# Attention kernel on one core: P times V of two blocks in a row at every second block, with four buffers of exponentials instead of two

## The chip, the core and the metric

The kernel runs on one core of a Trainium2 chip. The core has a matrix engine (PE, TensorE), a vector engine (DVE, VectorE), an activation engine (ACT, ScalarE), a general engine (POOL, GpSimd) and DMA queues (issued here by SP, SyncE). The engines run their own instruction streams in order and meet at semaphores. PE writes its products to PSUM, which has eight banks of 2 KB per partition; DVE and ACT read them from there. The metric is the device time of one execution in microseconds; before the change it is 294.55 us (median of 3 runs, 294.25 to 294.76).

## The reference, cut to what matters

Input x is 4 batches x 512 tokens x 128 channels, in fp32.

```
xn  = layernorm(x)
q   = (xn @ Wq + bq)            as 16 heads of 8
k   = ((xn @ Wk + bk) @ Wl + bl) as 16 heads of 8
v   = ((xn @ Wv + bv) @ Wl + bl) as 16 heads of 8
att = softmax(q k^T / sqrt(8)) @ v       for each batch and head
x   = x + layernorm(att @ Wo + bo)
# then a gated feed-forward part with a shift by one token
xr, xk = mu*xn + (1-mu)*previous token of xn      (xn = layernorm(x))
x   = x + layernorm(sigmoid(xr @ W_r^T) * (square(relu(xk @ W_k^T)) @ W_v^T))
```

## The kernel before

A batch has 16 heads in 4 groups (GH = 4 heads each) and 512 keys in 4 tiles of 128. A block is one group and one key tile: 16 blocks per batch (BLK = 16, block n has group n // 4 and tile n % 4), 64 blocks in all. In the text, E(0) to E(3) are the four score products of a block for its exponentials, one per head (`scores_for_exponentials`, line 1262: 128 keys x 512 queries, in bf16). They go to the two banks of psB in turn. X(0) to X(3) are the four exponentials of ACT (line 784), which read these banks and write pT, of which there are two buffers, one per block. M stands for the four score products for the maxima (`scores_for_maxima`, line 1243), which are done LEAD = 6 blocks ahead of their use. Two of them (u = 0) fill the first half of psA, two (u = 1) the second, and DVE takes the maximum over each half in one reduction: R(0) and R(1) (line 933). After four blocks POOL splits the maxima of a group into three bf16 parts in four steps (`split_maxima`, lines 493, 553, 557), PE transposes them (job "m"), ACT copies them and a DMA brings them into QS.

PV is `times_v` (line 1274): for one block, four products, one per head, of V (128 keys x 32 columns, of which 8 are the head's and one holds ones for the row sum) with pT (128 keys x 512 queries), in fp32. Each writes 32 partitions of the bank psO, and the four tiles of a group add up there. The chip has two matmul instructions for each of these fp32 products, so that a block's PV is eight in the trace: four column tiles, then the four again. After a group ACT copies psO to o_sb (`take_o`), PE transposes it (job "on") and DVE divides by the sums (`normalise`).

The order is written out by hand. On PE a block is

E(0), M, E(1), M, M, E(2), M, E(3), then PV of the block before.

Between these stand the jobs, by the table PE_AT with pairs (block, place): the transposes of the outputs of a group ("on"), of the maxima ("m"), and those of the feed-forward part of the batch before ("oT", "y", "x1T", "r", "kf", "f"). Place 0 is after the first half of M, place 1 after the third M, 2 after the fourth, 3 after E(3) and ahead of PV, 4 after PV. ACT_AT and DVE_AT set the same for the other engines: ACT does X(0), X(1), results, X(2), X(3) with results also ahead of X(0); DVE does R(0), work, R(1), work.

The waits that matter here are these. E(i) waits until the exponential two before it has been done (`e_rdy`), since psB has two banks. The first M of a half waits until the reduction of that half of the block before is done (`a_max`). X of block n waits until PV of the last block that used its pT buffer is done (`pv_done`). PV waits for the exponentials of its block (`e_rdy`), at a group's first tile also for V (`vg_rdy`) and for the copy of the group before out of psO (`o_tak`). For the last six blocks of the last batch there are no more M, and psA serves as two further banks for E.

Batch 0 has no feed-forward jobs, batches 1 and 2 run in a loop, the last is written out again.

Of the kernel before, what the change touches and what calls it, by code (L numbers as in the profile page):

```python
# [23 lines left out]
def sandwich_kernel(nc, x, Wq, bq, Wk, bk, Wv, bv, Wl, bl, Wo, bo, W_r, W_k, W_v, mu_r, mu_k, out):  # L24
# [4 lines left out]
    ACT = mybir.ActivationFunctionType  # L29
# [3 lines left out]
    NB, T, E = x.shape  # L33
    H = 16
    D = E // H
    P = 128
    NT = T // P
    GH = 4
    NG = H // GH
    BLK = NG * NT  # L40
# [11 lines left out]
    with ctx:  # L52
        def sb(name, shape, dt=fp32):
            return ctx.enter_context(nc.sbuf_tensor(name, shape, dt))
# [4 lines left out]
        def sem(name):  # L59
            return ctx.enter_context(nc.semaphore(name))  # L60
# [50 lines left out]
        MC = GH * NT  # L111
        mm = sb("mm", [P, P], bf16)
        mmT = sb("mmT", [PARTS * MC, P], bf16)
        pT = sb("pT", [P, 2, GH, T])
        o_sb = sb("o_sb", [P, T])
        rsum = sb("rsum", [P, NT, GH])
        oq = sb("oq", [P, NT, H, D])
# [106 lines left out]
        pv_done = sem("pv_done")  # L224
# [117 lines left out]
        def job_before(b, job, first, last):  # L342

            have = [j for j in JOBS if not (first and j[0] == "F") and not (last and j[0] == "L")]
            at = [j[1] for j in have].index(job)
            if not at:

                return (m_tak, 1) if first else (on_tak, b * NG - 1)
            _, _, taken, a, c = have[at - 1]
            return taken, b * a + c  # L350

        def later(n):

            return not isinstance(n, int) or n > 0
# [3 lines left out]
        def score_bank(n, i, last):  # L358

            if last and n >= TAIL and i >= 2:  # L360
                return psA[:, 0, i - 2, :]
            return psB[:, i % 2, :]
# [319 lines left out]
        def _(act):  # L682
# [54 lines left out]
            for t in range(NT):  # L737
                last = nc.scalar.copy(bout[:, t, :], psA[:, 1, 1, 0:E])
            last.then_inc(s_boc, 1)
            def take_first_maxima(_):  # L740
                take_maxima(0, psB[:, 0, :].bitcast(bf16))
# [36 lines left out]
            def exponentials(b, n, i, last):  # L778

                act.wait_ge(b_rdy, b * (BLK * GH) + (n * GH + i + 1))  # L780
                if n >= 2 or later(b):

                    act.wait_ge(pv_done, b * BLK + (n - 1))
                nc.scalar.activation(pT[:, n % 2, i, :], score_bank(n, i, last), ACT.Exp,  # L784
                                     scale=SCALE).then_inc(e_rdy, 1)

            def batch(b, first, last):
                for n in range(BLK):
                    take_results(b, n, 0, first, last)
                    exponentials(b, n, 0, last)  # L790
                    exponentials(b, n, 1, last)
                    take_results(b, n, 1, first, last)
                    exponentials(b, n, 2, last)
                    exponentials(b, n, 3, last)
# [60 lines left out]
            for u in range(2):  # L855
                act.wait_ge(z_fst, 2 * HALF * (u + 1))
                for t in z_tiles(u):
                    last = nc.scalar.activation(zf[:, t, :], f_sb[:, t, :], ACT.Identity, scale=-1.0,
                                                bias=mv_f[:, t, 0:1])
# [290 lines left out]
        def _(pe):  # L1150
# [52 lines left out]
            def job_m(n, bank=psM_b):  # L1203
                pe.wait_ge(m_p2, n + 1)
                nc.tensor.transpose(bank[:, 0:P], mm[:, :], ident_b[:, :]).then_inc(m_rdy, 1)  # L1205

            def job_on(n):
                pe.wait_ge(o_tak, n + 1)
                transposes(lambda t: o_sb[:, P * t:P * (t + 1)], on_rdy)
# [26 lines left out]
            def scores_for_maxima(e, a, g, h, u, j, free=False):  # L1236

                if u == 0 and j == 0 and h == 0:
                    pe.wait_ge(ld[g], (e + 1) * (16 * LW))
                if j == 0 and not free:  # L1240
                    pe.wait_ge(a_max, a * 2 + (u - 1))
                t = 2 * u + j
                score = nc.tensor.matmul(psA[:, u, j, :], QS[g][0:KMAX, h, P * t:P * (t + 1)],  # L1243
                                         KS[g][0:KMAX, h, :], start=True, stop=True)
                if j == 1:
                    score.then_inc(a_rdy, 1)

            def scores_for_exponentials(b, n, i, later_tile, last):

                g, t = n // NT, n % NT  # L1250
                if t == 0 and i == 0:
                    pe.wait_ge(m_in, b * (16 * NG) + 16 * (g + 1))
                if last and n >= TAIL and i >= 2 and n == TAIL:
                    if i == 2:
                        pe.wait_ge(a_max, 2 * BLK * NB)
                elif last and (n > TAIL or n == TAIL and i >= 2):

                    pe.wait_ge(e_rdy, b * (BLK * GH) + (n * GH + i - 3))
                elif later_tile:

                    pe.wait_ge(e_rdy, b * (BLK * GH) + (n * GH + i - 1))
                nc.tensor.matmul(score_bank(n, i, last), KS[g][0:KEXP, i, P * t:P * (t + 1)],  # L1262
                                 QS[g][0:KEXP, i, :], start=True, stop=True).then_inc(b_rdy, 1)

            def times_v(b, n, later_group):

                g, t = n // NT % NG, n % NT
                if t == 0:
                    pe.wait_ge(vg_rdy, b * NG + (n // NT + 1))
                    if later_group:  # L1270
                        pe.wait_ge(o_tak, b * NG + n // NT)
                pe.wait_ge(e_rdy, b * (BLK * GH) + GH * (n + 1))
                for i in range(GH):
                    last = nc.tensor.matmul(psO[QUAD * i:QUAD * (i + 1), :], Vg[:, g, t, i, :],  # L1274
                                            pT[:, n % 2, i, :], start=(t == 0), stop=(t == NT - 1))
                last.then_inc(pv_done, 1)

            job_xT(0)
# [2 lines left out]
            for j in range(2):  # L1281
                nc.tensor.matmul(psA[:, 1, 0, E * j:E * (j + 1)], w_T[:, T_WK + j, :], w_in[:, WL, :],
                                 start=True, stop=True).then_inc(s_wkl, 1)
            job_q(0)
            pe.wait_ge(s_vec, 16 * 7)
            for j in range(2):
                nc.tensor.matmul(psA[:, 1, 1, j:j + 1], w_in[:, WL, :], vec[:, V_BK + j:V_BK + j + 1],
                                 start=True, stop=True).then_inc(s_bkl, 1)
# [8 lines left out]
                             stop=True).then_inc(s_bo, 1)  # L1297
# [27 lines left out]
            def batch(b, first, last):  # L1325
                def jobs(n, place):

                    for kind, name, _, _, _ in JOBS:
                        if PE_AT[name] == (n, place) and not (first and kind == "F") \
                                and not (last and kind == "L"):  # L1330
                            pe.wait_ge(*job_before(b, name, first, last))
                            run_job(name)

                def run_job(name):
                    if name.startswith("on"):
                        job_on(b * NG + int(name[2:]))
                    elif name.startswith("m"):
                        job_m(b * NG + int(name[1:]))
                    else:
                        {"oT": job_oT, "y": job_y, "x1T": job_x1T, "r": job_r, "kf": job_kf,  # L1340
                         "f": job_f}[name](b - 1)

                for n in range(BLK):
                    ahead = n + LEAD

                    def for_maxima(u, j):
                        if ahead < BLK or not last:
                            scores_for_maxima(b + ahead // BLK, b * BLK + ahead, ahead // GH % NG,
                                              ahead % GH, u, j)

                    def for_exponentials(i):
                        scores_for_exponentials(b, n, i, i > 1 or n > 0 or not first, last)

                    for_exponentials(0)
                    for_maxima(0, 0)
                    for_exponentials(1)
                    for_maxima(0, 1)
                    jobs(n, 0)
                    for_maxima(1, 0)
                    jobs(n, 1)  # L1360
                    for_exponentials(2)
                    for_maxima(1, 1)
                    jobs(n, 2)
                    for_exponentials(3)
                    if first and n == 0:
                        pe.wait_ge(k_tak, 2 * NB)
                        pe.wait_ge(q_tak, 2 * NB)
                    jobs(n, 3)
                    if n or not first:
                        times_v_before(b, n, first)  # L1370
                    jobs(n, 4)

            def times_v_before(b, n, first):
                if n:
                    times_v(b, n - 1, n > 1 or not first)
                else:
                    times_v(b - 1, BLK - 1, True)

            batch(0, True, False)
            with pe.Fori(1, NB - 1) as i:  # L1380
                batch(i, False, False)
            batch(NB - 1, False, True)
            e = NB - 1
            times_v(e, BLK - 1, True)


# [79 lines left out]
```

## Time and profile before

| | |
|---|---|
| time, median of 3 runs | 294.55 us |
| span of the profiled execution, first to last instruction | 292.1 us |
| PE busy | 257.6 us, 88% of the span |
| DVE busy | 218.2 us, 75% |
| ACT busy | 180.4 us, 62% |
| POOL busy | 108.1 us, 37% |
| 512 PV matmuls (line 1274), busy together | 69.1 us |
| 128 reductions for the maxima (line 933), mean of one | 1216 ns |
| 244 exponentials (line 784), mean of one | 597 ns |

The page gives no time of the profiled execution other than its span, which is 2.45 us shorter than the median of the runs. Matmuls overlap: one takes about 0.38 us from its start to its end, but the next one starts 0.22 us after it, so starts say more than durations. In the timeline a row stands for several instructions in a row where it says x2 or more; its time is from the first start to the last end.

### The profile page before, as it was taken

Reading aid. Unit: us, or ns where it says so; the run is one execution under the profiler, and the core shown is the slowest. Engines: PE = TensorE matmul, PEld = TensorE weight load, DVE = VectorE, ACT = ScalarE, POOL = GpSimd, SP = SyncE. Lnnn points to the kernel's source line nnn. Section 1 sums busy time; section 2 is a strip of 40 time slices with the busy share of each in tenths; the row PEclk is TensorE's granted clock in tenths of the full one; section 3 lists DMA queues with packets and bytes.
Section 4 is the critical chain, followed back from the end, with each engine's and each line's share of the span. In section 5 each row is a group of like instructions: output and inputs, shape, how many; then the busy total and the mean of one; then the engine's idle time right before and its main releaser. Section 6 shows DMA issues by size and latency. Waiting matters only on the chain.

```text
span 292.1 us, 4845 instructions
## 1 busy us (share of the span) xinstructions
PE 257.6 (88%) x1379; PEld 100.2 (34%) x1379; DVE 218.2 (75%) x384; ACT 180.4 (62%) x351; POOL 108.1 (37%) x236
## 2 busy tenths in 40 slices
PE   7764883099999999999999999999999999898980
PEld 2441541022323232432433334233333433333560
DVE  2695494065888787989889889988998988763545
ACT  2334350566787867687776776777677678695041
POOL 4897370321001011066321344552117155324522
PEclk9686699558999999999999999999999999999798
DMA  4331133160111111110101121010102000000101
GB/s 108 108 109 77 77 125 123 52 198 2 61 39 66 42 46 56 33 77 19 68 27 57 33 88 49 33 66 20 68 12 103 17 1 2 4 1 0 36 2 36
DMA packets 13045, 15.64 MB, mean 54 GB/s; under 512 B 2529, under 2 KB 10722, under 8 KB 13026
## 3 DMA queue, kind: packets, MB, share of 16 engines
q1 hardware_dynamic: 12450, 15.15, 15.5%
q10 hardware_dynamic: 576, 0.26, 0.3%
q8 instruction: 9, 0.15, 0.2%
q14 instruction: 10, 0.08, 0.1%
HBM read 11.01 MB, written 4.19 MB: 52 GB/s over the span
## 4 chain that ended last, share of the span: by engine, by line
PE 72%; DMA 9%; DVE 8%; SPq 4%; ACT 3%; issue 3%; POOL 1%; POOLq 0%; DVEq 0%; ACTq 0%
PE psO L1274 20%; PE psB L1262 20%; PE psA L1243 17%; DMA q_scr<-qp 4%; DVE mx L933 4%; PE psM L1167 3%; PE psM L1173 3%; SPq L382 3%; DMA KS<-k_scr 3%; PE psA L1154 2%; PE psB L1396 1%; DVE er L996 1%; DMA x_all<-in_L_attn_x_dram 1%; PE psO L1186 1%; SPq L401 1%
## 5 line engine op out<-in xcount | busy, mean ns | idle before, releaser
L933 DVE TENSOR_REDUCE mx<-psA 128x2 f32<-128x1024 f32 x128 | 150.8, 1216 | 45.2 <-PE psA L1243 44.8
L784 ACT ACTIVATE pT<-psB 128x512 f32<-128x512 f32 x244 | 133.1, 597 | 41.2 <-PE psB L1262 40.4
L1262 PE MATMUL psB<-QS,KS 99*128 99x512 bf16 x244 | 94.7, 393 | 12.3 <-DMA QS<-mmT 11.9
L1243 PE MATMUL psA<-KS,QS 96*128 96x512 bf16 x256 | 90.7, 391 | 5.7 <-DMA KS<-k_scr 4.4
L1274 PE MATMUL psO<-pT,Vg 128*32 128x512 f32 x512 | 69.1, 611 | 0.4
L1262 PEld LDWEIGHTS psB<-QS,KS 99*128 99x128 bf16 x244 | 23.6, 98 | 92.0 <-ACT pT L784 57.3
L1243 PEld LDWEIGHTS psA<-KS,QS 96*128 96x128 bf16 x256 | 25.2, 100 | 28.7 <-DVE mx L933 6.2
L493 POOL TENSOR_TENSOR mm<-mx,one 128x16 bf16<-128x16 f32 x16 | 3.5, 217 | 43.2 <-DVE mx L933 43.2
L1274 PEld LDWEIGHTS psO<-pT,Vg 128*32 128x32 f32 x512 | 10.2, 108 | 21.8 <-issue 16.9
L532 POOL TENSOR_TENSOR Vg<-v_st,one 128x128 f32<-128x128 f32 x16 | 6.3, 399 | 28.0 <-PE psO L1274 28.0
L703 ACT ACTIVATE qf<-psO,vec 128x512 f32<-128x512 f32 x4 | 2.7, 687 | 18.0 <-DMA q_scr<-qp 13.4
L1154 PE MATMUL psA<-warm 128*128 128x512 bf16 x36 | 11.4, 482 | 1.2 <-DVE warm L905 1.2
L996 DVE RECIPROCAL er<-rr 128x128 f32<-128x128 f32 x12 | 10.7, 924 | 2.3 <-POOL rr L639 2.3
L760 ACT COPY o_sb<-psO 128x512 f32<-128x512 f32 x15 | 8.8, 590 | 4.4 <-PE psO L1274 4.4
L884 DVE TENSOR_SCALAR xh<-x_all,mv_x,rs_x 128x128 f32<-128x128 f32 x16 | 8.0, 653 | 1.9 <-POOL rs_x L500 1.8
L1173 PE MATMUL psM<-ident,o_sb 128*128 128x128 f32 x60 | 9.0, 272 | 0.0
L694 ACT COPY xhT<-psB 128x512 f32<-128x512 f32 x4 | 2.3, 586 | 10.6 <-PE psB L1179 10.6
L520 POOL TENSOR_TENSOR qr<-qf,qp 128x512 f32<-128x512 f32 x3 | 3.5, 1155 | 14.1 <-ACT qp L704 14.1
L1173 PEld LDWEIGHTS psM<-ident,o_sb 128*128 128x128 f32 x60 | 7.5, 141 | 2.9
L506 POOL TENSOR_TENSOR ve_y<-mv_y,eps 128x4 f32<-128x4 f32 x3 | 0.6, 202 | 20.9 <-DVE mv_y L875 20.9
L506 POOL TENSOR_TENSOR ve_f<-mv_f,eps 128x4 f32<-128x4 f32 x3 | 0.6, 201 | 20.5 <-DVE mv_f L875 20.5
L734 ACT COPY mmT<-psM 48x128 bf16<-48x128 bf16 x15 | 3.8, 254 | 4.9 <-PE psM L1205 4.9
(179 smaller groups left out, 293.8 us busy)
## 6 DMA issues: line engine op xcount, KB each, us to landing
QS<-q_scr SPq DMA_DIRECT2D x48, 96.0 KB
KS<-k_scr SPq DMA_DIRECT2D x16, 288.0 KB
q_scr<-qp SPq DMA_DIRECT2D x12, 128.0 KB, 2.3
k_scr<-kp SPq DMA_DIRECT2D x12, 128.0 KB, 2.3
x_all<-in_L_attn_x_dram SPq DMA_DIRECT2D x4, 256.0 KB, 3.4
out_dram<-out_sb SPq DMA_DIRECT2D x3, 256.0 KB, 4.0
QS<-mmT SPq DMA_DIRECT2D x16, 12.0 KB
out_dram<-out_sb SPq DMA_DIRECT2D x2, 128.0 KB, 1.8
```

What stands on the lines that cost most here:

```text
L382: sp.dma_start(scr[b, i, :, :, :].rearrange("d h n -> h d n"), parts[:, b % 2, i, :]).then_inc(written[b], 16)
L760: nc.scalar.copy(o_sb[:, :], psO[:, :]).then_inc(o_tak, 1)
L784: nc.scalar.activation(pT[:, n % 2, i, :], score_bank(n, i, last), ACT.Exp, scale=SCALE).then_inc(e_rdy, 1)
L884: last = nc.vector.tensor_scalar(xh[:, b, t, :], x_all[:, b, E * t:E * (t + 1)], mv_x[:, b, t, 0:1], rs_x[:, b, t:t + 1], ALU.subtract, AL ...
L933: nc.vector.tensor_reduce(out=mx[:, g % 2, c:c + 2], in_=psA[:, u, :, :], axis=AX.X, op=ALU.max).then_inc(a_max, 1)
L996: nc.vector.reciprocal(er[:, E * t:E * (t + 1)], rr[:, E * t:E * (t + 1)])\
L1154: nc.tensor.matmul(psA[:, 1, 0, :], warm[:, 0:P], warm[:, :], start=True, stop=True)
L1167: last = nc.tensor.matmul(psM[:, E * t:E * (t + 1)], lhs[:, P * t:P * (t + 1)], rhs, start=True, stop=True)
L1173: last = nc.tensor.transpose(psM[:, P * t:P * (t + 1)], src(t), ident[:, :])
L1243: score = nc.tensor.matmul(psA[:, u, j, :], QS[g][0:KMAX, h, P * t:P * (t + 1)], KS[g][0:KMAX, h, :], start=True, stop=True)
L1262: nc.tensor.matmul(score_bank(n, i, last), KS[g][0:KEXP, i, P * t:P * (t + 1)], QS[g][0:KEXP, i, :], start=True, stop=True).then_inc(b_rdy, 1)
L1274: last = nc.tensor.matmul(psO[QUAD * i:QUAD * (i + 1), :], Vg[:, g, t, i, :], pT[:, n % 2, i, :], start=(t == 0), stop=(t == NT - 1))
```

## The change

pT gets four buffers (PT = 4), block n uses buffer n % 4, and the exponentials of block n wait for PV of block n - 4 instead of n - 2. PE does no PV at the end of odd blocks. At the end of an even block n it does those of blocks n - 2 and n - 1, one behind the other. After the last block of the last batch it does blocks 14 and 15.

```
-        pT = sb("pT", [P, 2, GH, T])
+        PT = 4
+        pT = sb("pT", [P, PT, GH, T])
...
-                if n >= 2 or later(b):
+                if n >= PT or later(b):
-                    act.wait_ge(pv_done, b * BLK + (n - 1))
-                nc.scalar.activation(pT[:, n % 2, i, :], score_bank(n, i, last), ACT.Exp,
+                    act.wait_ge(pv_done, b * BLK + (n - PT + 1))
+                nc.scalar.activation(pT[:, n % PT, i, :], score_bank(n, i, last), ACT.Exp,
...
-                                            pT[:, n % 2, i, :], start=(t == 0), stop=(t == NT - 1))
+                                            pT[:, n % PT, i, :], start=(t == 0), stop=(t == NT - 1))
...
-                    if n or not first:
+                    if n % 2 == 0 and (n or not first):
                         times_v_before(b, n, first)
                     jobs(n, 4)
             def times_v_before(b, n, first):
-                if n:
-                    times_v(b, n - 1, n > 1 or not first)
-                else:
-                    times_v(b - 1, BLK - 1, True)
+                for back in (2, 1):
+                    if n:
+                        times_v(b, n - back, n - back > 0 or not first)
+                    else:
+                        times_v(b - 1, BLK - back, True)
...
             e = NB - 1
+            times_v(e, BLK - 2, True)
             times_v(e, BLK - 1, True)
```

PE, batch 0, from E(2) of block 1 to the end of block 2, before. L1262 is E, L1243 is M, L1274 is PV:

```order
L1262 MATMUL psB<-QS,KS 128x512
L1243 MATMUL psA<-KS,QS 128x512
L1262 MATMUL psB<-QS,KS 128x512
L1274 MATMUL psO<-pT,Vg 32x512 x4
L1262 MATMUL psB<-QS,KS 128x512
L1243 MATMUL psA<-KS,QS 128x512
L1262 MATMUL psB<-QS,KS 128x512
L1243 MATMUL psA<-KS,QS 128x512 x2
L1262 MATMUL psB<-QS,KS 128x512
L1243 MATMUL psA<-KS,QS 128x512
L1262 MATMUL psB<-QS,KS 128x512
L1274 MATMUL psO<-pT,Vg 32x512 x4
```

The same stretch of the changed kernel, whose lines are one further down (L1263 is E, L1244 is M, L1275 is PV):

```order
L1263 MATMUL psB<-QS,KS 128x512
L1244 MATMUL psA<-KS,QS 128x512
L1263 MATMUL psB<-QS,KS 128x512 x2
L1244 MATMUL psA<-KS,QS 128x512
L1263 MATMUL psB<-QS,KS 128x512
L1244 MATMUL psA<-KS,QS 128x512 x2
L1263 MATMUL psB<-QS,KS 128x512
L1244 MATMUL psA<-KS,QS 128x512
L1263 MATMUL psB<-QS,KS 128x512
L1275 MATMUL psO<-pT,Vg 32x512 x8
```

The four PV products that stood between two blocks are gone; E(3) of the odd block is followed directly by E(0) of the even one, and eight products stand behind the even one.

PE, the end of the last batch before, from the E of block 15 with the waits of each instruction (L1173 is the transposes "on2", L1389 the first work of the end):

```order
L1262 MATMUL psB<-QS,KS 128x512 [waits e_rdy] x2
L1173 MATMUL psM<-ident,o_sb 128x128 [waits o_tak,f_tak]
L1173 MATMUL psM<-ident,o_sb 128x128 x3
L1262 MATMUL psA<-QS,KS 128x512 [waits e_rdy] x2
L1274 MATMUL psO<-pT,Vg 32x512 [waits e_rdy]
L1274 MATMUL psO<-pT,Vg 32x512 x3
L1274 MATMUL psO<-pT,Vg 32x512 [waits e_rdy]
L1274 MATMUL psO<-pT,Vg 32x512 x3
L1389 MATMUL psA<-ident,o_sb 128x128 [waits z_o]
```

And in the changed kernel:

```order
L1263 MATMUL psB<-QS,KS 128x512 [waits e_rdy] x2
L1174 MATMUL psM<-ident,o_sb 128x128 [waits o_tak,f_tak]
L1174 MATMUL psM<-ident,o_sb 128x128 x3
L1263 MATMUL psA<-QS,KS 128x512 [waits e_rdy] x2
L1275 MATMUL psO<-pT,Vg 32x512 [waits e_rdy]
L1275 MATMUL psO<-pT,Vg 32x512 x3
L1275 MATMUL psO<-pT,Vg 32x512 [waits e_rdy]
L1275 MATMUL psO<-pT,Vg 32x512 x3
L1392 MATMUL psA<-ident,o_sb 128x128 [waits z_o]
```

Here nothing has moved: the last two blocks were multiplied one behind the other before too. The order of DVE, ACT, POOL and SP is unchanged throughout; on ACT only the value that `pv_done` is compared with is another.

## Rows read from the trace of the kernel before

**Rows 1.** The page: busy PE in total, and the granted clock in 40 slices.
```profile
PE 257.6 (88%) x1379; PEld 100.2 (34%) x1379; DVE 218.2 (75%) x384; ACT 180.4 (62%) x351; POOL 108.1 (37%) x236
PEclk9686699558999999999999999999999999999798
```
**Rows 2.** Busy time by stretch: batch 0, batch 1, end of batch 3.
```profile
core 0: us, PE busy (x) PEld busy (x) DVE busy (x) ACT busy (x) POOL busy (x), PEclk, DMA share, GB/s
67.00:114.70 47.70, 47.39 (x268) 14.47 (x265) 37.70 (x37) 36.43 (x71) 4.39 (x17) 0.99 0.13 44
114.70:168.60 53.90, 53.70 (x310) 19.50 (x310) 48.40 (x76) 39.25 (x77) 19.54 (x50) 1.00 0.13 46
248.20:267.60 19.40, 18.10 (x115) 6.06 (x113) 11.48 (x34) 15.19 (x31) 5.11 (x10) 1.00 0.01 2
```
**Rows 3.** Waits over the whole span: total us, times, longest us.
```profile
PEld psB L1262 <- ACT pT L784: 57.3, 107, 0.8
PEld psA L1243 <- DVE mx L933: 6.2, 12, 0.9
```
**Rows 4.** Timeline, block 7 of batch 0: start us, us, engine, line, tiles, count.
```profile
84.20 1.06 PE L1274 MATMUL psO<-pT,Vg 128*32 128x512 f32 x8
85.19 0.39 PE L1262 MATMUL psB<-QS,KS 99*128 99x512 bf16 x1
85.62 2.17 ACT L784 ACTIVATE pT<-psB 128x512 f32<-128x512 f32 x4 [0.71 <-PE psB L1262]
85.86 0.59 PE L1243 MATMUL psA<-KS,QS 96*128 96x512 bf16 x2
86.28 2.35 DVE L933 TENSOR_REDUCE mx<-psA 128x2 f32<-128x1024 f32 x2 [0.53 <-PE psA L1243]
86.76 0.39 PE L1262 MATMUL psB<-QS,KS 99*128 99x512 bf16 x1
87.08 1.07 PE L1274 MATMUL psO<-pT,Vg 128*32 128x512 f32 x8
88.08 0.39 PE L1262 MATMUL psB<-QS,KS 99*128 99x512 bf16 x1
```
**Rows 5.** Timeline, PE: the second half of one PV of the last batch.
```profile
260.95 0.64 PE L1274 MATMUL psO<-pT,Vg 128*32 128x512 f32 x4
261.40 0.61 PE L1274 MATMUL psO<-pT,Vg 128*32 128x512 f32 x4
```
**Rows 6.** Timeline, batch 1, an M of block 12 that waited for a reduction.
```profile
150.26 1.16 DVE L933 TENSOR_REDUCE mx<-psA 128x2 f32<-128x1024 f32 x1
151.05 0.82 PE L1243 MATMUL psA<-KS,QS 96*128 96x512 bf16 x2
```
**Rows 7.** Timeline, batch 1: blocks 3 to 6, starts of E(0), maxima of block 5.
```profile
119.06 0.38 PE L1262 MATMUL psB<-QS,KS 99*128 99x512 bf16 x1
126.33 0.39 PE L1262 MATMUL psB<-QS,KS 99*128 99x512 bf16 x1
127.41 2.36 DVE L933 TENSOR_REDUCE mx<-psA 128x2 f32<-128x1024 f32 x2 [0.61 <-PE psA L1243]
130.73 0.22 POOL L557 TENSOR_TENSOR mm<-mr,mm 128x16 bf16<-128x16 f32 x1
131.21 0.22 PE L1205 MATMUL psM<-ident_b,mm 128*128 128x128 bf16 x1
132.58 0.39 PE L1262 MATMUL psB<-QS,KS 99*128 99x512 bf16 x1
```
**Rows 8.** Timeline, batch 1: from job r to block 13.
```profile
145.38 1.16 PE L1167 MATMUL psM<-w_T,xr 128*128 128x128 f32 x8
146.58 0.60 ACT L776 ACTIVATE er<-psM 128x512 f32<-128x512 f32 x1 [0.77 <-PE psM L1167]
148.59 1.76 DVE L996 RECIPROCAL er<-rr 128x128 f32<-128x128 f32 x2
153.46 0.39 PE L1262 MATMUL psB<-QS,KS 99*128 99x512 bf16 x1
```
**Rows 9.** Timeline, end of the last batch: the last exponentials and PV.
```profile
265.31 1.09 ACT L784 ACTIVATE pT<-psA 128x512 f32<-128x512 f32 x2
265.32 2.20 PE L1274 MATMUL psO<-pT,Vg 128*32 128x512 f32 x16
```
**Rows 10.** Timeline, PE, batch 0: the first PV.
```profile
65.12 1.94 PE L1274 MATMUL psO<-pT,Vg 128*32 128x512 f32 x8
66.99 0.61 PE L1262 MATMUL psB<-QS,KS 99*128 99x512 bf16 x1
```

## The prediction

> **What bounds the kernel now.** I read the page first. PE is busy 88% of the span, and its clock is granted in full over most of it [rows 1]. By stretch it is tighter: through the batches PE is busy 47.4 of 47.7 us and 53.7 of 53.9 us, at 0.99 to 1.00 of the clock [rows 2]. So in the steady part PE's work follows itself and every step saved on PE would be a gain, provided that nothing else is late. Then the waits: E stood behind an exponential 107 times, never over 0.8 us, M behind a maximum only 12 times [rows 3]. Most of the 57.3 us for E is PV's own running time (the weight load of E waits in parallel with it), so the sum says little; the timeline does.
>
> In the timeline a plain block goes from E(0) at 85.19 to the next E(0) at 88.08, 2.89 us [rows 4]. Matmuls start 0.22 us apart (three steps from 85.19 to 85.86), E(3) to PV is 0.32, PV to the next E(0) is 85.19 - 84.20 = 1.00. In the same block DVE has two reductions, one 1.14 after the other (2.35 less one of 1.21), 2.28 us in all, and ACT four exponentials at 0.49 (1.09 less 0.60) [rows 9], 1.96 us. Both are below 2.89, but not by much, and both work from two buffers: psA has two halves, psB two banks. PE can run ahead of DVE by one half only.
>
> **What the change saves.** Within one PV the second four start 0.45 after the first four (261.40 - 260.95) [rows 5]. Then the next 128-column product comes 1.00 - 0.45 = 0.55 after the start of the last four, 0.10 more than another four would, and the four start 0.32 after E(3) instead of 0.22, another 0.10 [rows 4]. These two 0.10 are the price of going from 128 to 32 columns and back. Two PVs in one go take 1.00 + 2 x 0.45 = 1.90 us and one 0.32; apart they take 2 x (0.32 + 1.00) = 2.64, and joined 1.90 + 0.32 + 0.22 (the plain step where the other stood) = 2.44. That saves 0.20 per pair. There are 31 pairs that were apart (the last of the 32 was joined before: x16 in rows 9), so 31 x 0.20 = 6.2 us at most. The joint between two PVs isn't in the trace without a wait: at the end the second one starts 2.20 - 1.06 = 1.14 after the first, held by the last exponential. Its bounds are nothing extra (0.45, as inside a PV) and the whole 0.20 (as if drained in between). I take 0.45, since it is again four column tiles behind four, with a new set of weights as the second half of a PV also has; the other end is 31 x 0.20 = 6.2 us worse.
>
> The Trainium skill, page "TensorEngine Tiling (Array Packing)", key properties under "Tiling Modes", says that changing the tiling mode drains TensorE. The two 0.10 us of the rows agree with it, and by it alone the result would be 6.2 us faster. The same page, "PSUM Bottleneck" under "Performance Considerations", warns that tiling speeds TensorE but not the reading out of PSUM. That speaks against the change, and the next part is what it comes to here.
>
> The wait of X on PV goes: block n needs PV of n - 4, done at the latest at the end of block n - 2. It did not hold anything before either (X(0) starts 0.43 after E(0)), worth 0. The copies of psO (`take_o`) and V's groups hang on the last PV of a group, at the end of an even block, in the same place as before: 0.
>
> **What it costs: the cover of the readers.** PV is the stretch in which DVE and ACT catch up. It now comes as 1.90 us once in two blocks, and by then PE's two halves and two banks are full, so the readers run out of work. In the two blocks that follow each other without PV, PE could go at 8 x 0.22 = 1.76 us a block, but DVE needs 2.28. I work it out with these links: E to X 0.43 and X to the E of its bank 0.65 (X(1) at 85.62 + 0.49 = 86.11, E(3) at 86.76), second M of a half to R 0.42 (85.86, 86.28) [rows 4], start of R to the M that it holds 1.23 (150.26; the second M of the row is at 151.05 + 0.82 - 0.38 = 151.49) [rows 6].
>
> Odd block, E(0) at 0 just after a PV: second M of the first half 0.67, R(0) 1.09, R(1) 1.09 + 1.14 = 2.23; X at 0.43, 0.92, 1.53, 2.02. Even block: E(0) waits for X(2): 2.17. Its first M 2.39, E(1) waits for X(3) to 2.67, second M 2.89, R(0) 3.37. The third M waits for R(1) of the odd block: 2.23 + 1.23 = 3.46. Then E(2) 3.68, M 3.90, E(3) 4.12, PV 4.44, next odd E(0) 4.44 + 1.90 = 6.34. Before, the pair took 2 x 2.89 = 5.78. **So a plain pair is 0.56 us slower**, although its switches are cheaper by 0.20: the stall is 0.78 us. After PV nothing is owed (the last R ends 5.7), so it repeats in each pair.
>
> Jobs change that, as cover or as work for the readers. Pairs are named by their blocks, batch 1 and 2:
> (3,4): jobs oT (0.44) and y (1.0) stand in the odd block and cover DVE and ACT; full gain. Before 126.33 - 119.06 = 7.27 [rows 7], less 0.23 (the 0.20 and 0.03 of waits).
> (5,6): the transposes "on0" (0.44) cover part, but job m2 stands ahead of E(3) of block 6 and needs POOL's four steps after R(1) of block 5. R(1) is at 127.41 + 1.14 = 128.55, POOL ends at 130.95, 2.40 later, and m2 at 131.21 didn't wait [rows 7]. Now R(1) at 2.23 gives m2 at 2.23 + 2.40 + about 0.15 = 4.78; E(3) 4.84, PV 5.15, end 7.05, against 132.58 - 126.33 = 6.25 before: +0.80.
> (11,12): the two reciprocals of the gate stand ahead of R(1) of block 11 on DVE. The chain from job r (145.38) over ACT (146.58), POOL and DVE (148.59) to R(1) (150.26) and the M that it holds (151.49) takes 6.11 us and is not shortened [rows 6, 8]. Before, PV stood inside it as cover; now it does not. From that M: E(2) 0.22, M 0.44, E(3) 0.66, PV 0.98, end 2.88. So 6.11 + 2.88 = 8.99 from r, against 153.46 - 145.38 = 8.08 [rows 8]: +0.91.
> The others come by the same table with their own jobs, as estimates: (1,2) +0.43 (ACT's copy is in it), (7,8) +0.32 (a wait of 0.17 for x1T was there before), (9,10) +0.60 (m3 waits for POOL as m2, PV right behind it), (13,14) +0.18 (f covers, m4 waits), (15,0) +0.46 (DVE's division stands ahead of R(1)). Sum of a middle batch: 0.43 - 0.23 + 0.80 + 0.32 + 0.60 + 0.91 + 0.18 + 0.46 = 3.47.
>
> Batch 0 has no feed-forward jobs: plain pairs (3,4), (7,8), (11,12) 3 x 0.56, (5,6) +0.84, (9,10) +0.60, (13,14) +0.79 (m4 waits, no f), (15,0) +0.28. For (1,2) +0.10: the first PV ran at half clock in 66.99 - 65.12 = 1.87 us [rows 10], and moved behind block 2 it meets the full clock. Sum 4.3. Batch 3: pairs as in a middle batch up to (7,8) without its (15,0) at the end, which is counted at its start; +0.43 - 0.23 + 0.80 + 0.32 = 1.32. From block 10 no M is left, four banks are open, and the jobs kf and f cover ACT: twice -0.20; (9,10) +0.25. Together 1.2. The end is unchanged: the last PV waits for X(3) of block 15 (265.31 + 0.49 = 265.80; PV 266.46) [rows 9] as before.
>
> Sum: 4.3 + 2 x 3.47 + 1.2 = 12.4 us on the profiled execution (span 292.1, to 304.5). The rest of the time, 2.45 us outside the span, stays: 294.55 + 12.4 = **307.0 us**.
>
> **Rivals.**
> 1. Faster: the switches go and the readers keep up. For it: PE fills the steady part, DVE is busy 37.7 of 47.7 us in batch 0 and ACT 36.4 [rows 2], so on average both have room. Against it: the room lies where PV was, and two halves of psA do not carry it over. It would need M's third product to wait no more than 0.2 us in the even block where I find 0.78 of stall. Price: 294.55 - 6.2 = 288.4 us. It decides from a stall below 0.20 a pair.
> 2. The stall is half as long as I think (a link is shorter, or jobs cover more): the pair's 0.78 becomes about 0.4, which leaves +0.2 x 31 = 6 less the middle batches' extra: 295 to 300 us, say 298. For it: the estimates of five kinds of pairs are. Against it: 1.23 and 1.14 are rows.
> 3. The change doesn't do what it says: between the two PVs PE waits as if the mode changed, so nothing is saved, and the stalls come on top: 307.0 + 6.2 = 313.2. For it: the joint is not in the trace. Against it: no change of columns takes place there.
>
> **Chances.** My forecast 0.75, with its own range 301 to 311.5 (the waits of m2, m3, m4 are 0.4 to 0.5 each at ten places, so 4 us less if POOL's result isn't awaited; 4 us more if a joint costs half of its bound and a chain like (11,12) slips further). Rival 1 0.10, rival 2 0.07, rival 3 0.08. The range from 299.5 to 312.0 leaves out rival 1, a part of 2 and most of 3. A measurement of this kernel tells about 0.2% (0.6 us) from no change. Faster 0.10, same 0.03 (the edge between 1 and 2), slower 0.87.
>
> **What would show it.** Right: PV rows as x16 with about 1.90 us to the next E; a plain pair of 6.3 us; M (line 1244) waiting for DVE about once a pair, in the even block (12 times in all before); DVE and ACT idle in each PV; PE no longer busy 99% of a batch; (3,4) shorter than 7.27 us. Wrong: plain pairs of 5.6 us (rival 1), 2.1 us or more from the first PV to E (rival 3), a granted clock below 0.99 in the batches, which I don't expect, as PE's longest new idle stretch is near 1 us; or X waiting for `pv_done`.

## The result and the profile after

The changed kernel takes 308.7 us (median of 4 runs) against 294.65 us; the ratio is 1.048, with a 95% interval of 1.0458 to 1.0503. It is slower by 14.05 us. One of the four runs took 313.37 us; the ratio is formed without it. I had forecast 307.0 us, with a range from 299.5 to 312.0. The profiled execution took 308.78 us with a span of 307.0, 14.9 more than the span before. Outside its span lie 1.8 us; for the kernel before, where I had the median alone to set against the span, I had 2.45. Later runs of the kernel before have 1.8 outside the span too (294.68 with 292.9), so the span of 292.1 belonged to an execution of some 293.9 us. The 0.65 that I added too much hides a part of the miss: 2.5 us in the span (307.0 for 304.5), 1.7 in the time.

The page after: busy time, the clock in 40 slices, and the groups of the reductions and of PV (L934 and L1275 are L933 and L1274 of before).

```profile
PE 257.4 (84%) x1379; PEld 102.9 (34%) x1379; DVE 216.9 (71%) x384; ACT 180.4 (59%) x351; POOL 107.8 (35%) x236
...
PEclk9797897569999999999999999999999999799897
...
L934 DVE TENSOR_REDUCE mx<-psA 128x2 f32<-128x1024 f32 x128 | 150.5, 1215 | 58.7 <-PE psA L1244 58.4
L1275 PE MATMUL psO<-pT,Vg 128*32 128x512 f32 x512 | 62.9, 608 | 0.1
```

The work on every engine is what it was [rows 1]. PV's busy time fell from 69.1 to 62.9 us, which is the overlap at the joints; PE's sum did not fall with it (257.6 and 257.4), which fits with there being more waits: a product ahead of a wait adds its whole 0.38 us to the sum, one in a row its step of 0.22. All that was added to the span is idle time. By stretch (batch 0 from block 3 on, then a batch's length from 117 us on, and four microseconds late in batch 3):

```profile
core 0: us, PE busy (x) PEld busy (x) DVE busy (x) ACT busy (x) POOL busy (x), PEclk, DMA share, GB/s
70.00:117.00 47.00, 43.03 (x243) 13.72 (x240) 33.87 (x34) 32.77 (x64) 4.16 (x16) 1.00 0.13 45
117.00:174.60 57.60, 53.44 (x311) 20.31 (x310) 48.59 (x76) 39.35 (x78) 19.04 (x49) 1.00 0.12 42
264.00:268.00 4.00, 3.98 (x21) 1.47 (x22) 1.75 (x10) 1.23 (x3) 0.00 (x0) 0.61 0.01 3
```

Batch 1 took 53.9 us with PE busy 53.7 [rows 2]; now such a stretch is 57.6 us with PE busy 53.4. PE has the same work and now waits about 4 us in each batch. In the last row the clock is at 0.61 inside batch 3, which was not so before; more of it below.

A plain pair of blocks after, 7 and 8 of batch 0, which answers to [rows 4]. Columns: start us, us, engine, line, tiles, count, and in brackets the idle time before it and what ended it:

```profile
82.95 0.39 PE L1263 MATMUL psB<-QS,KS 99*128 99x512 bf16 x1
...
84.03 4.62 DVE L934 TENSOR_REDUCE mx<-psA 128x2 f32<-128x1024 f32 x4 [1.88 <-PE psA L1244]
...
85.20 0.38 PE L1263 MATMUL psB<-QS,KS 99*128 99x512 bf16 x1 [0.30 <-ACT pT L785]
...
86.44 0.39 PE L1244 MATMUL psA<-KS,QS 96*128 96x512 bf16 x1 [0.20 <-DVE mx L934]
...
87.11 0.38 PE L1263 MATMUL psB<-QS,KS 99*128 99x512 bf16 x1
...
87.42 1.92 PE L1275 MATMUL psO<-pT,Vg 128*32 128x512 f32 x16
...
89.27 0.39 PE L1263 MATMUL psB<-QS,KS 99*128 99x512 bf16 x1
```

This is the table of the prediction, row by row. From E(0) at 82.95: R(0) at 1.08 (1.09 was worked out), E(0) of the even block at 2.25 after a wait for ACT (2.17), its third M at 3.49 after a wait for DVE (3.46), E(3) at 4.16 (4.12), PV at 4.47 (4.44), the next E(0) at 6.32 (6.34). DVE does its four reductions in one go, 4.62 us, and had been idle for 1.88 us before them, which is PV's time: its work in the two halves of psA did not last until PE wrote the next.

The weight loads (PEld) show how the sixteen go in four groups of four. Those of the first two groups come at once, those of the third as the second group starts (87.87), those of the fourth as the third starts (88.30):

```profile
87.42 0.16 PEld L1275 LDWEIGHTS psO<-pT,Vg 128*32 128x32 f32 x8 [0.43 <-issue]
87.87 0.13 PEld L1275 LDWEIGHTS psO<-pT,Vg 128*32 128x32 f32 x4 [0.30 <-ACT pT L785]
...
88.30 0.13 PEld L1275 LDWEIGHTS psO<-pT,Vg 128*32 128x32 f32 x4 [0.30 <-issue]
```

So the groups start 0.45 and 0.43 us apart, across the joint (87.87 to 88.30) as inside a PV, and the pair of PVs takes 89.27 - 87.42 = 1.85 us. I had 1.90. The joint costs nothing; the saving is about 0.24 per pair, not 0.20 (0.25 at (3,4) in the table below, 0.24 in the runs that follow).

The waits over the whole span, which answer to [rows 3]:

```profile
PEld psB L1263 <- ACT pT L785: 39.9, 95, 0.9
...
PEld psA L1244 <- DVE mx L934: 16.2, 30, 1.6
```

M stood behind a reduction 30 times and 16.2 us in all, against 12 times and 6.2 us.

Pair by pair, from E(0) of the odd block to E(0) of the next odd block (starts in the two timelines, us):

| pair | before | after | change | forecast |
|---|---|---|---|---|
| batch 0: (1,2) | 8.74 | 8.30 | -0.44 | +0.10 |
| (3,4) | 5.76 | 6.53 | +0.77 | +0.56 |
| (5,6) | 6.19 | 6.98 | +0.80 | +0.84 |
| (7,8), (11,12) | 5.77 | 6.32 | +0.55 each | +0.56 |
| (9,10) | 6.22 | 6.77 | +0.55 | +0.60 |
| (13,14) | 6.02 | 6.77 | +0.75 | +0.79 |
| (15,0) | 6.53 | 6.81 | +0.28 | +0.28 |
| batch 1: (1,2) | 6.44 | 6.89 | +0.45 | +0.43 |
| (3,4) | 7.27 | 7.02 | -0.25 | -0.23 |
| (5,6) | 6.25 | 6.93 | +0.68 | +0.80 |
| (7,8) | 6.51 | 6.82 | +0.31 | +0.32 |
| (9,10) | 7.29 | 8.01 | +0.72 | +0.60 |
| (11,12) | 7.08 | 7.94 | +0.86 | +0.91 |
| (13,14) | 6.76 | 7.11 | +0.35 | +0.18 |
| (15,0) | 6.35 | 6.82 | +0.47 | +0.46 |
| batch 3: (9,10) | 7.60 | 10.09 | +2.49 | +0.25 |
| (11,12), (13,14) | 4.87, 4.82 | 4.99, 5.07 | +0.12, +0.25 | -0.20 each |

Batch 2 is as batch 1 but for (15,0), 6.17 before and 6.82 after (+0.65, forecast +0.46). The pairs (1,2) to (7,8) of batch 3 came at +0.40, -0.25, +0.80 and +0.32, for +0.43, -0.23, +0.80 and +0.32.

### The profile page after: what moved, and what is told of

It reads as the page before. It is cut to its first block, busy times and chain, and to the rows that moved or that the text cites. A ratio compares the mean times of both kernels' runs of the same rounds, so it can differ in the third digit from the quotient of the medians.

```text
span 307.0 us, 4839 instructions
## 1 busy us (share of the span) xinstructions
PE 257.4 (84%) x1379; PEld 102.9 (34%) x1379; DVE 216.9 (71%) x384; ACT 180.4 (59%) x351; POOL 107.8 (35%) x236
## 4 chain that ended last, share of the span: by engine, by line
PE 55%; DVE 17%; DMA 9%; issue 7%; ACT 4%; POOL 4%; SPq 3%; POOLq 0%; DVEq 0%; ACTq 0%
PE psO L1275 19%; DVE mx L934 12%; PE psB L1263 12%; PE psA L1244 11%; DMA q_scr<-qp 3%; PE psM L1168 3%; DMA KS<-k_scr 3%; SPq L383 2%; ACT pT L785 2%; PE psA L1155 2%; POOL mm L494 2%; DMA QS<-mmT 1%; PE psM L1174 1%; DVE er L997 1%; PE psB L1399 1%
## 5 line engine op out<-in xcount | busy, mean ns | idle before, releaser
L934 DVE TENSOR_REDUCE mx<-psA 128x2 f32<-128x1024 f32 x128 | 150.5, 1215 | 58.7 <-PE psA L1244 58.4
L1263 PE MATMUL psB<-QS,KS 99*128 99x512 bf16 x244 | 95.0, 394 | 20.0 <-DMA QS<-mmT 13.1
L1244 PE MATMUL psA<-KS,QS 96*128 96x512 bf16 x256 | 91.9, 393 | 8.5 <-DVE mx L934 5.1
L1275 PE MATMUL psO<-pT,Vg 128*32 128x512 f32 x512 | 62.9, 608 | 0.1
L1263 PEld LDWEIGHTS psB<-QS,KS 99*128 99x128 bf16 x244 | 23.8, 98 | 82.1 <-ACT pT L785 39.9
L1244 PEld LDWEIGHTS psA<-KS,QS 96*128 96x128 bf16 x256 | 25.1, 100 | 34.3 <-DVE mx L934 16.2
L1275 PEld LDWEIGHTS psO<-pT,Vg 128*32 128x32 f32 x512 | 13.3, 109 | 29.0 <-issue 20.8
L885 DVE TENSOR_SCALAR xh<-x_all,mv_x,rs_x 128x128 f32<-128x128 f32 x16 | 7.1, 598 | 1.9 <-POOL rs_x L501 1.8
```

What stands on the lines that cost most here:

```text
L885: last = nc.vector.tensor_scalar(xh[:, b, t, :], x_all[:, b, E * t:E * (t + 1)], mv_x[:, b, t, 0:1], rs_x[:, b, t:t + 1], ALU.subtract, AL ...
L934: nc.vector.tensor_reduce(out=mx[:, g % 2, c:c + 2], in_=psA[:, u, :, :], axis=AX.X, op=ALU.max).then_inc(a_max, 1)
```

## The experiments

Repeated runs of one and the same kernel scattered by some microseconds in these sets (before: 290.51 to 296.31 us over 23 runs), and the kept traces, one of each kernel, put most of it into the first blocks and the end, where the clock's changes fall in other places each time: the part behind the last block's E(0) was between 26.6 and 31.3 us in the five traces of complete work, the pair (1,2) of batch 0 between 7.85 and 9.09. In between, pairs that an edit leaves alone agree within 0.1 us from trace to trace, except where the clock fell inside batch 3. So beside the times I compare the stretch from E(0) of block 3 of batch 0 to E(0) of block 15 of batch 3, called the middle: 193.54 us before, 209.27 after (+15.73). Each middle is that of one trace.

**The four buffers alone.**

```
+        PT = 4
+        pT = sb("pT", [P, PT, GH, T])      (and the wait and n % PT as in the change)
         if n or not first:
             times_v_before(b, n, first)     as before: one PV a block
```

> The changed kernel's four buffers of exponentials alone: PV after every block as before, X waits for PV of block n - 4. Theory (the loss is the missing cover of DVE and ACT, the buffers are worth nothing): 294.65 us, within 0.3. Rival A (the buffers, or where they lie in memory, cost something of their own): slower, up to 14 us. Rival B (X was held by pv_done before): faster than 294.0.

Measured: 294.07 us, ratio 1.0008 (0.9966 to 1.0049). The middle is 193.32 us. Plain pairs are 5.77 as before; only the pairs around a batch's start moved, (15,0) from 6.53 to 6.25 in batch 0 and from 6.35 to 6.25 in batch 1, (1,2) from 6.44 to 6.51 in batches 1 and 2. In block 0 of batch 1, X(0) started 0.79 us after E(0) before and 0.51 with the four buffers. So the buffers cost nothing, and with two of them X did wait for PV at a batch's start: that was worth 0.2 us in the middle, not nothing as in the prediction. Rival A is out. Another effect of the buffers in the kernel with pairs wasn't tried.

**Two PVs in a row only where the readers are covered.**

```
-                    if n % 2 == 0 and (n or not first):
+                    if (n or not first) and (first or n != 3):
                         times_v_before(b, n, first)
...
-                for back in (2, 1):
+                for back in ((2, 1) if n == 4 and not first else (1,)):
```

> Two PVs in a row at one place of a batch only, blocks 2 and 3 at the end of block 4 in the batches 1 to 3, where the jobs oT and y stand between; everywhere else one PV a block. Theory: the saved switches are real where the readers are covered; in the changed kernel this pair is 7.02 and 6.94 us long against 7.27 and 7.19 before, so 3 x 0.24 = 0.7 us faster: 293.9 us. Rival (a row of sixteen costs something elsewhere, as a late start of what follows it): 294.65 or slower.

Measured: 293.49 us, ratio 0.9994 (0.9956 to 1.0031), which tells nothing at this scatter. The trace does:

```profile
118.57 0.38 PE L1263 MATMUL psB<-QS,KS 99*128 99x512 bf16 x1
...
123.73 1.92 PE L1275 MATMUL psO<-pT,Vg 128*32 128x512 f32 x16
125.59 0.39 PE L1263 MATMUL psB<-QS,KS 99*128 99x512 bf16 x1
```

The pair (3,4) takes 125.59 - 118.57 = 7.02 us, against 7.27 [rows 7]; in batch 2 it is 7.02 for 7.26 and in batch 3 6.94 for 7.19. No pair behind it is longer. The middle is 192.61 us, 0.71 less than with the four buffers alone, that is 0.24 each. This is the version with complete work whose middle is shortest (0.93 us below the kernel before), but its time could not be told from that kernel's.

**The transposes of the maxima behind PV.**

```
-  "m2": (6, 2)   "m3": (10, 3)   "m4": (14, 3)      PE_AT
+  "m2": (6, 4)   "m3": (10, 4)   "m4": (14, 4)
-  "m3": (10, 1)                                     ACT_AT
+  "m3": (11, 0)
```

> The changed kernel with the transposes of the maxima m2, m3, m4 moved behind the pair of PVs (place 4 instead of 2, 3, 3; ACT's copy of m3 to block 11). Theory (in the changed kernel they wait for POOL at 10 or more places, 0.2 to 0.5 us each, and 1.75 us in block 10 of the last batch, where the clock then fell): gain of 1.4 us in batch 0, 1 us each in batches 1 and 2, 2.5 us in the last, less 0.2 us for each group whose first E then waits for the DMA of the maxima (up to 11): 304 to 305.5 us, and no half clock inside batch 3. Rival (the place of m does not matter, the reductions set the pace): 308.7 us within 0.5.

Measured: 302.67 us, ratio 1.0358 (1.0264 to 1.0453), lower than either theory. The middle is 204.68, 4.6 us less than after, which is within the 3.2 to 4.7 of the theory; the rest of the gain is luck of the clock, since the end took 26.61 us in this trace and 28.29 after. The 4.6 came otherwise than forecast: 1.0 in batch 0, only 0.2 in each of batches 1 and 2, and 3.1 in batch 3. Pairs (5,6) fell from 6.98 to 6.42 (batch 0) and from 6.93 to 6.49, (13,14) from 6.77 to 6.39 and from 7.11 to 6.95, (9,10) of batch 3 from 10.09 to 7.45. In batches 1 and 2 (9,10) did not fall (8.07). And a group's first E now waits for the DMA of the maxima, as in block 8 of batch 3:

```profile
250.80 0.39 PE L1263 MATMUL psB<-QS,KS 99*128 99x512 bf16 x1
251.94 0.39 PE L1263 MATMUL psB<-QS,KS 99*128 99x512 bf16 x1 [0.75 <-DMA QS<-mmT]
```

There E(0) comes 1.14 after E(3) of block 7. It made (7,8) longer by 0.12 to 0.32. The clock was full from 78 to 273 us, past the last block's E(0) (same columns as the stretches above):

```profile
78.00:273.00 195.00, 180.95 (x1064) 67.61 (x1068) 158.41 (x242) 138.70 (x270) 61.34 (x154) 1.00 0.11 39
```

The next six leave work out, so their times say what a reader costs, not what a kernel could do. Each reduction covers 256 (or 128) of the 512 keys of its two tiles, each exponential 256 (or 128) of the 512 queries.

**Half reductions, with the change.**

```
-                                        in_=psA[:, u, :, :],
+                                        in_=psA[:, u, :, 0:T // 2],
```

> The changed kernel, each reduction for the maxima over 256 of the 512 keys (the other half is left out). Theory: a reduction then starts 0.6 after the other instead of 1.14, M no longer waits, and a plain pair is held by ACT's two banks alone: 4.09 + 1.90 = 5.99 us instead of 6.33; total 297 to 300 us, still slower than before. Rival (the pair of PVs costs by itself, apart from the readers): plain pair stays 6.3 us and the time 308.

```profile
83.74 0.39 PE L1263 MATMUL psB<-QS,KS 99*128 99x512 bf16 x1
...
86.00 0.38 PE L1263 MATMUL psB<-QS,KS 99*128 99x512 bf16 x1 [0.30 <-ACT pT L785]
...
87.87 1.92 PE L1275 MATMUL psO<-pT,Vg 128*32 128x512 f32 x16
...
89.73 0.39 PE L1263 MATMUL psB<-QS,KS 99*128 99x512 bf16 x1
```

299.17 us, ratio 1.0161 (1.0075 to 1.0248). The plain pair is 89.73 - 83.74 = 5.99 us, as forecast: DVE's wait is gone, ACT's is left. The middle is 199.94, 9.3 us less than after; (9,10) of batch 3 again ran its PVs at half clock (9.53).

**Half reductions, without the change.** The same edit in the kernel before.

> The kernel before with reductions over 256 of the 512 keys, as a control. Theory (PE is the bound of a block there, DVE has room): plain block stays 2.89 us; only where DVE's gate stands in the chain a little is gained: 293.5 to 294.6 us. Rival (DVE's reductions hold the kernel before as well): a block well under 2.89 and 290 us or less.

292.16 us, ratio 0.9923 (0.9881 to 0.9965). Plain pairs stay at 5.77 us, the middle falls by 1.2 us to 192.33, most of it at (9,10) of batch 3 (7.60 to 7.02) and at the gate, (11,12) from 7.08 to 6.97. The time came out below the 293.5 to 294.6 that I expected: DVE does not hold a plain block of the kernel before, but at a few other places it costs 1.2 us.

**Half exponentials, with the change.**

```
-                nc.scalar.activation(pT[:, n % PT, i, :], score_bank(n, i, last), ACT.Exp,
+                nc.scalar.activation(pT[:, n % PT, i, 0:T // 2],
+                                     score_bank(n, i, last)[:, 0:T // 2], ACT.Exp,
             x_normalise(3)
+            nc.vector.memset(pT[...], 1.0)
```

> The changed kernel with exponentials over 256 of the 512 queries (the other half of pT keeps a constant written once early). Theory: DVE's two halves alone already hold a plain pair: third M of the even block at 2.23 + 1.23, so 6.3 us as now; total 307 to 308.5 us. Rival (ACT's two banks are what holds it): plain pair under 6.1 us, total under 303.

```profile
82.78 0.39 PE L1264 MATMUL psB<-QS,KS 99*128 99x512 bf16 x1
...
85.14 0.10 PEld L1245 LDWEIGHTS psA<-KS,QS 96*128 96x128 bf16 x1 [0.25 <-DVE mx L935]
...
86.28 0.39 PE L1245 MATMUL psA<-KS,QS 96*128 96x512 bf16 x1 [0.30 <-DVE mx L935]
...
87.25 1.92 PE L1276 MATMUL psO<-pT,Vg 128*32 128x512 f32 x16
89.11 0.39 PE L1264 MATMUL psB<-QS,KS 99*128 99x512 bf16 x1
```

305.23 us, ratio 1.0351 (1.0245 to 1.0456). The plain pair is 6.33 us, unchanged: with ACT out of the way, the first M of the even block (85.14) and the third (86.28) wait for DVE, and the third one starts as late as before. Its total came out below my 307 to 308.5: the middle is 206.47, 2.8 us less than after, of which 1.63 is (9,10) of batch 3, where the PVs ran at full clock in this trace (8.46 us), and 0.36 and 0.43 are the last two pairs of batch 3, where ACT is the reader that matters.

**Both halves, with and without the change.** The two edits above together.

> The changed kernel with half reductions and half exponentials together. Theory: no reader is late, PE is full: a plain pair 16 x 0.22 less one step + 0.32 + 1.90 = 5.5 to 5.6 us, less than two blocks of the kernel before (5.77); total 288 to 291 us, so that the saved switches show. Rival (the switches saved are not worth 0.20 a pair): 293 us or more.

> The kernel before with half reductions and half exponentials, as a control for the one with both halves and paired PVs. Theory: PE full as it was, block 2.85 to 2.89 us, total 292.5 to 294.3 us, some 4 to 6 us slower than the paired one with the same halves. Rival (the readers are the bound in the kernel before too): equal to or faster than the paired one.

289.15 us (ratio 0.9835, 0.9751 to 0.992) with the change, 287.47 us (0.9777, 0.9694 to 0.9861) without. The plain pairs are 5.73 and 5.69 us. The time of the first is within the 288 to 291 of its theory, the rest missed. The pair was to be 5.5 to 5.6 and the kernel before to be 4 to 6 us slower than the paired one; instead they are nearly level on the pair and the paired kernel is slower in the middle, 193.02 to 188.25. The rival of the second run came true: its middle is 5.3 us below that of the kernel before with full readers, 4.1 below that with half reductions alone. So ACT too held the kernel before, hardly in a plain pair (5.77 to 5.69) but in others, as (11,12) of batches 1 and 2 (6.97 to 6.58). A wait is left in the paired kernel:

```profile
82.68 0.88 PE L1264 MATMUL psB<-QS,KS 99*128 99x512 bf16 x2
```

The x2 are E(3) of the odd block and E(0) of the even one. The second starts 0.88 - 0.38 = 0.50 after the first instead of 0.22, since E(0) needs the bank of E(2), three products earlier only. That is the price of two blocks' E side by side. Of the 4.8 us in the middle, 2.5 are again (9,10) of batch 3 (9.52 against 7.02, some 1.6 of it the half clock again), and 0.56 each are (11,12) in batches 1 and 2, the gate.

**Quarters, with and without the change.** The same edits with T // 4 for T // 2.

> The changed kernel with reductions over 128 of the 512 keys and exponentials over 128 of the 512 queries (the rest is left out). With halves a plain pair was 5.73 us, still 0.2 above PE's own work, because E(0) of the even block stands right behind E(2) and E(3) of the odd one. Theory: with quarters this wait nearly goes too, a plain pair is 5.46 to 5.55 us. Rival (the rest lies in PE or in the row of PVs, not in the readers): 5.7 us stays.

> Control: the kernel before with the same quarters. Theory: PE has no wait left with halves already, so a plain pair stays 5.68 us, about 0.2 longer than the paired one with quarters, which is what the saved switches are worth. Rival: it falls as well and the paired kernel has no advantage left.

284.87 us with the change, 286.3 us without (two runs each; their intervals, 0.9429 to 1.0042 and 0.9485 to 1.0084, overlap). The middles are 186.96 and 187.79. The plain pairs, first with the change, then without:

```profile
80.16 0.39 PE L1264 MATMUL psB<-QS,KS 99*128 99x512 bf16 x1
...
81.70 0.78 PE L1264 MATMUL psB<-QS,KS 99*128 99x512 bf16 x2
...
83.93 1.92 PE L1276 MATMUL psO<-pT,Vg 128*32 128x512 f32 x16
85.79 0.39 PE L1264 MATMUL psB<-QS,KS 99*128 99x512 bf16 x1
```

```profile
80.19 0.39 PE L1263 MATMUL psB<-QS,KS 99*128 99x512 bf16 x1
...
84.88 1.07 PE L1275 MATMUL psO<-pT,Vg 128*32 128x512 f32 x8
85.88 0.39 PE L1263 MATMUL psB<-QS,KS 99*128 99x512 bf16 x1
```

5.63 against 5.69 us. The wait at E(0) of the even block is still 0.18 (0.78 - 0.38 = 0.40 instead of 0.22); 0.06 + 0.18 = 0.24 is the value of the switches, and the halves give the same (0.28 of wait less 0.04). In this trace X(2) starts 0.42 after E(2), takes 0.28, and E(0) comes 0.14 behind it: 0.84, against three steps of 0.22. As an estimate from these, an exponential would have to take 0.1 us or less for the wait to go. So the paired kernel is behind with half the readers' work and ahead by 0.8 us in the middle with a quarter; their times cannot be told apart. The pair was to be 5.46 to 5.55 and came out 0.08 above, by this one wait. The control's pair stayed as expected (5.69 for 5.68), but it was to be 0.2 longer than the paired one and is 0.06 longer.

## Why the prediction was right, and where it was not

**The lost cover.** It holds. The plain pair came out at 6.32 us for 6.34, with each wait at its place. Half reductions brought it to 5.99, half exponentials alone left it at 6.33, and the same half reductions left the plain pairs of the kernel before at 5.77. So DVE's two halves of psA set the plain pair after the change, ACT's two banks are next, and neither set it before. The middle lost 15.7 us to the change with full readers, 4.8 us with halves (193.02 - 188.25), and gained 0.8 us with quarters. Outside the plain pairs PE was not the only bound before: both halves took 5.3 us out of the middle of the kernel before. And the stall of 0.78 is a slip in the prediction's own terms: 0.56 and 0.20 are 0.76, which changed nothing in the sum.

**The switches saved.** The mechanism holds, the term was a little small: 0.24 a pair instead of 0.20. Rival 3 (the joint costs) is out by the groups of PV at 0.43 to 0.45 us. Where jobs cover the readers, at (3,4), the pair is 0.25 shorter, in the changed kernel as well as where it is the only pair. Rival 1 needed the stall below 0.20 a pair; it was 0.24 + 0.55 = 0.79. Rival 2 (half of it) is out by the same rows. A rival that I had not named is the change of type, from bf16 to fp32, which comes with the change of columns. The kernel before settles it, with the fp32 products of 128 columns of job f between two M of block 13 in batch 1:

```profile
154.12 0.38 PE L1243 MATMUL psA<-KS,QS 96*128 96x512 bf16 x1
154.34 1.05 PE L1167 MATMUL psM<-w_T,kact 128*128 128x128 f32 x8
155.23 0.38 PE L1243 MATMUL psA<-KS,QS 96*128 96x512 bf16 x1
```

The first of the eight starts 0.22 after M, the usual step, and M starts 0.89 after it, which is eight of their own steps of 0.11. The change of type costs nothing here, so the 0.10 each way is that of the columns. The Trainium skill's rule on draining ("TensorEngine Tiling (Array Packing)", "Key Properties" under "Tiling Modes") agrees in direction with the 0.24 us here; no run tells draining from another cost of going to 32 columns and back. The Trainium skill's "PSUM Bottleneck" on the same page agrees too, though not as a rate, since DVE and ACT were idle more than before (71% and 59% busy): what lacked was banks to read from while PV ran.

**The m jobs.** The wait for POOL was there, as worked out. Block 6 of batch 1:

```profile
134.25 0.22 POOL L558 TENSOR_TENSOR mm<-mr,mm 128x16 bf16<-128x16 f32 x1
...
134.53 0.23 PE L1206 MATMUL psM<-ident_b,mm 128*128 128x128 bf16 x1 [0.30 <-POOL mm L558]
...
134.93 1.92 PE L1275 MATMUL psO<-pT,Vg 128*32 128x512 f32 x16
```

PE takes 0.06 from POOL's end, where I had 0.15; that is most of the difference between +0.68 and +0.80. Moving these jobs behind PV took 4.6 us out of the middle, 2.6 of it at (9,10) of batch 3.

**What failed: (9,10) of batch 3.** I had +0.25 and it was +2.49 us. PE there, before:

```profile
252.08 0.22 PE L1205 MATMUL psM<-ident_b,mm 128*128 128x128 bf16 x1 [1.15 <-POOL mm L557]
252.22 1.07 PE L1274 MATMUL psO<-pT,Vg 128*32 128x512 f32 x8
```

PE, then POOL, after:

```profile
262.05 0.60 PE L1263 MATMUL psA<-QS,KS 99*128 99x512 bf16 x2
264.02 0.22 PE L1206 MATMUL psM<-ident_b,mm 128*128 128x128 bf16 x1 [1.37 <-POOL mm L558]
264.17 3.03 PE L1275 MATMUL psO<-pT,Vg 128*32 128x512 f32 x16
267.13 1.69 PE L1168 MATMUL psM<-w_T,xr 128*128 128x128 f32 x8
268.65 0.60 PE L1263 MATMUL psB<-QS,KS 99*128 99x512 bf16 x2
```

```profile
262.66 0.55 POOL L494 TENSOR_TENSOR mm<-mr,one 128x16 bf16<-128x16 f32 x1
263.29 0.59 POOL L558 TENSOR_TENSOR mm<-mr,mm 128x16 bf16<-128x16 f32 x1
```

Two things. First, block 10 has no M, so PE is early at m3 and waits for POOL, whose last two steps take 0.55 and 0.59 here (the last one took 0.22 in [rows 7]). Both steps run while DVE works on xr and xk, 0.74 us each, in all the traces; that this slows them was not tried. The wait was there before too (m3 came 5.46 us after E(0) of block 9 in both timelines), but PV of block 8 then stood ahead of it, and now it follows: 0.9 us, the size seen with half exponentials (8.46 against 7.60). The prediction has no working for its +0.25, only m2's 4.78 for a block with M. Second, the granted clock fell to half behind this idle stretch: the pair of PVs took 267.13 - 264.17 = 2.96 us instead of 1.85, and r took 1.52 instead of 1.00, 1.6 us in all. A clock below 0.99 in the batches was one of my signs of being wrong, and I did not expect it, with PE's longest new idle stretch near 1 us; it was 1.37 (1.15 before, in the same place).

**ACT at the end of batch 3.** For (11,12) and (13,14) I took kf and f as enough cover, -0.20 each. They were +0.12 and +0.25; with half exponentials both are 4.63 and 4.64, that is -0.24 and -0.18. ACT was the reader that I had forgotten there: with four banks open it still has eight exponentials of about 0.49 to do for two blocks. In block 12 X(0) started 1.27 us after E(0), before 0.43.

**Smaller ones.** (3,4) of batch 0 was +0.77 instead of +0.56: blocks 3 and 4 now follow so closely that E(0) of block 4 waits for the maxima's DMA. It comes 2.79 us after E(0) of block 3, against 2.25 in a plain pair, and the pair is 0.21 longer than a plain one:

```profile
72.22 0.39 PE L1263 MATMUL psB<-QS,KS 99*128 99x512 bf16 x1 [0.84 <-DMA QS<-mmT]
```

The first blocks went the other way: to E(0) of block 3 the changed kernel was 0.93 us earlier, 0.44 of it in (1,2) of batch 0; I had it 0.10 later. I take that for luck: the part ahead of block 3 took from 69.0 to 71.1 us in the traces with full exponentials, whatever the kernel, by the places where the clock changed. In sum the misses (+3.0 in batch 3, -1.0 at the start, +0.5 in the rest) make 14.9 us of the 12.4 that I had in the span. Without the lucky start the sum would have been 3.5 us short.

## What to carry to other kernels

Work that engages only one engine is also the time in which the others catch up: before it is gathered into longer pieces, count how much work its readers still have at its start and compare it with the piece and the time until their next buffer is full. Here DVE had 1.23 us of reductions left when PV began (87.42 to 88.65), PV took 1.85, and the next full half came about 1.1 us behind it. Gather where other work stands in the thinned stretch (the one kind of pair that gained, 0.25 us, was such a place), and look at every job that sits right ahead of the piece, since the whole piece now waits behind it.

## What I had not expected of the hardware

- An idle stretch of PE of 1.37 us, at the end of four microseconds (260 to 264) in which it was busy for 2.29, was followed by a clock of 0.61 over the next 4 us in the changed kernel. At the same place the clock fell behind 0.98 us of idle time with half reductions and behind 1.24 with both halves (pairs of 9.53 and 9.52 us), but not behind 1.37 with half exponentials (8.46), 1.09 with quarters (7.62) or 1.15 in the kernel before. So the length of the stretch alone does not decide; what does was not tried.
- In a row of column-tiled products the third group of four starts 0.43 us after the second, a little less than the 0.45 between the first and the second, so that two PVs take 1.85 us and not 1.90.
- The scatter of the whole kernel (5.8 us for one kernel) was larger than most of the differences that the experiments were after (0.7 to 4.8 us in the middle); pairs of blocks in the traces agreed within 0.1 us and decided what the times could not.
